# Attention and mixture-of-experts layer on one core: three fp32r passes for fp32 products, another order around them, and scatters in pairs

## The chip, the cores and the metric

The kernel runs on one core of a Trainium2 chip. The core has TensorE (PE: matmuls; PEld: its weight loads), VectorE (DVE), ScalarE (ACT), GpSimd (POOL) and SyncE (SP, which here issues DMAs), and 16 DMA engines. The engines run programs of their own and meet at semaphores. The metric is the device time of one execution in microseconds; lower is better.

## The reference

One pre-norm transformer block in fp32 on 4 x 1024 tokens of 256 values:

```python
x = x + attn(layernorm(x))      # 16 heads of 16, causal window of 64, softmax
x = x + ffn(layernorm(x))

# ffn(x): 8 experts of width 128, two chosen per token, plus a shared one of width 256
scores = sigmoid(x @ gate_w.T + lb_bias)
topw, topi = top_k(scores, 2);  topw = topw / (topw.sum(-1, keepdims=True) + 1e-08)
for e in range(8):
    m = topi == e
    wmean = (topw * m).sum() / maximum(m.sum(), 1)      # one weight for all of an expert's tokens
    y = silu(x @ gate[e].T) * (x @ up[e].T) @ down[e].T
    out = out + where(m.any(-1)[:, None], y * wmean, 0)
out = out + silu(x @ shared_gate.T) * (x @ shared_up.T) @ shared_down.T
```

## The kernel before

The program is written engine by engine; the order on each engine is the order in which its functions are called, and every hand-over is a semaphore. No scheduler moves anything. It has four stages.

**Sweep.** 16 groups of 256 tokens, each of 4 blocks of 64 queries (64 blocks in all). `step(g, ..., old, ahead)` does group g; iteration n works on three blocks at once. On PE it issues the scores of block b+1, the P·V product of block b-1 (`pv_of`, 16 pairs of small matmuls), a piece of the next group's projections (q in iteration 0, k in 1, v in 2), the row-maximum correction of block b (`shift_of`), the transposition of the maxima of b+1 (`maxima_T`), the transposition of the P·V result (`pvT_of`, which waits for ScalarE's copy `pv_copy`), the output projection of the group before (`wo_of`, iterations 1 and 2) and the transposition of o (`oT_of`). VectorE takes the maxima of b+1 out of PSUM, makes the negated maxima in two bf16 parts, and SyncE's queue loads them as a row (`load_mrow`, two DMAs) for `shift_of` of b+1. VectorE also does layer norms, residuals, o, and the router's ranking (`comparisons`, `ranks`) for a group two or three behind. GpSimd does the power of the variances (`rstd_of`), computes where each token's row goes (`places`), and from group 4 on scatters the rows of the group four behind to the experts' lists in DRAM: `scatter` issues four indirect DMAs in a row, 128 rows of 1032 bytes each. SyncE loads one set of feed-forward weights per step (`load_weights`).

**Epilogue.** The last groups are routed, the tile table (which expert has which of the 72 tiles) is made, and between that PE does the first ten units of the shared expert. A unit is `gate_up` (four products) and `down` (two) for 256 tokens and half of the shared width.

**Tiles.** 72 tiles of 128 rows; tile t has on PE: two transpositions of its rows, two products for gate and up, one transposition of the hidden values, one product for down, spread over four rounds (`rows_T` of t+2, `tile_gate_up` of t+1, `hidden_T` of t, `tile_down` of t-1). VectorE copies the transposed rows and multiplies, ScalarE does silu, copies the transposed hidden values and scales the result, GpSimd scatters it to `y_rows` in DRAM, one indirect DMA a tile.

**Tail.** The remaining 22 shared units; two rows per token come back from `y_rows` (`load_experts_rows`), GpSimd adds the two, VectorE adds them to `xs` (`combined`), SyncE stores the group.

All products are plain fp32. One product in the code is `eng.matmul(out, lhsT, rhs)` with 128x128 weights and 256 moving columns; the trace has two records for each. In the names of the trace, `ps` is PSUM, `wA` the attention weights (and in the tiles the transposed rows and hidden values), `wF` the feed-forward weights, `yT`, `zT` and `oT` the transposed activations, `probs` the softmax, `pvs` the copied P·V.

GpSimd's part of a step before the change:

```python
if g >= GPB:
    places(g - GPB, place)
    scatter(g - GPB, place)
...
if old:
    if g > GPB:
        eng.wait_ge(s_sc[(g - 1) % GPB], 64 * ((g - 1) // GPB))
    rstd_of(1, g)
```

## Time and profile before

| | |
|---|---|
| time, median of 3 runs | 613.49 us (612.69 to 614.48) |
| the profiled execution | 616.98 us, span from first to last instruction 615.2 us |
| PE matmul busy | 555.0 us, 90% |
| PE weight loads busy | 417.2 us, 68% |
| VectorE busy | 354.0 us, 58% |
| ScalarE busy | 289.5 us, 47% |
| GpSimd busy | 218.4 us, 36% |
| mean granted TensorE clock | 0.968 of full speed |
| chain that ended last | PE 71%, VectorE 13%, unknown queue 6%, ScalarE 4% |

A record of a matmul overlaps the next one, so busy time is the union of records; the distance between records in a stream is the cost of one. An interval in brackets behind an instruction is the time for which its engine sat idle before it, and behind the arrow stands what ended that.

### The profile page before, as it was taken

The page shows a single profiled execution, that of the slowest core. Times are in us where ns is not written, and L with a number is a line of the kernel's source. Part 1 is how long each engine was busy: PE and PEld are TensorE (multiplying, and loading weights), DVE is VectorE, ACT ScalarE, POOL GpSimd, SP SyncE. Part 2 cuts the span into 40 slices and gives each one's busy share as a digit, 9 for nine tenths or more (in the row PEclk, how much of TensorE's full clock was granted, in tenths as well). Part 3 has the DMA queues.
Part 4 walks back from the last instruction along what each step waited for, and adds up shares of the span by engine and source line. Part 5 has one row for each costly group of instructions (what it writes and reads, how often), then busy time and mean ns, then how long its engine had stood idle before and what let it go on. Part 6 is the DMA issues. An engine that isn't in the chain of part 4 may idle for free.

```text
span 615.2 us, 14456 instructions
## 1 busy us (share of the span) xinstructions
PE 555.0 (90%) x4969; PEld 417.2 (68%) x4969; DVE 354.0 (58%) x1084; ACT 289.5 (47%) x650; POOL 218.4 (36%) x384
## 2 busy tenths in 40 slices
PE   7699999989898898898898987898999999999995
PEld 4466766666566565565575664786888887868884
DVE  4456577666465575675665567268555554533454
ACT  3366665645445555455455563221555554541110
POOL 4000012342240431422413423662456555555620
PEclk9899999999798998999999999698999999999999
DMA  7400000210201101112101101115455554518753
GB/s 249 164 3 3 2 2 4 62 45 20 63 23 40 52 20 55 37 27 63 36 2 38 36 2 38 70 57 159 135 152 162 153 159 134 157 58 301 247 147 126
DMA packets 37862, 50.79 MB, mean 83 GB/s; under 512 B 9244, under 2 KB 28063, under 8 KB 37792
## 3 DMA queue, kind: packets, MB, share of 16 engines
q1 hardware_dynamic: 31264, 33.02, 17.7%
q0 software_dynamic: 6528, 16.86, 8.3%
q8 instruction: 42, 0.69, 0.5%
q14 instruction: 28, 0.23, 0.1%
HBM read 27.36 MB, written 23.27 MB: 82 GB/s over the span
## 4 chain that ended last, share of the span: by engine, by line
PE 71%; DVE 13%; another core or an unknown queue 6%; ACT 4%; issue 3%; DMA 2%; POOL 1%; DVEq 0%; SPq 0%; POOLq 0%; ACTq 0%
PE ps L774 10%; PE ps L694 7%; PE ps L525 6%; PE ps L491 5%; PE ps L791 5%; PE ps L576 5%; PE ps L511 5%; PE ps L501 4%; DVE rmax L997 4%; PE ps L704 3%; PE ps L554 3%; PE ps L562 3%; PE ps L536 3%; PE ps L766 2%
## 5 line engine op out<-in xcount | busy, mean ns | idle before, releaser
L997 DVE TRANSPOSE_TENSOR_REDUCE rmax<-ps 128x32 f32<-128x1024 f32 x64 | 79.5, 1242 | 62.8 <-PE ps L525 61.0
L459 POOL DMA_INDIRECT y_rows<-vm,dest x72 | 70.2, 976 | 63.5 <-issue 40.1
L367 POOL TENSOR_TENSOR rstd<-mv,epsb 128x2 f32<-128x2 f32 x32 | 6.2, 193 | 241.6 <-DVE mv L982 241.6
L868 ACT ACTIVATE probs<-ps 128x1024 f32<-128x1024 f32 x64 | 65.7, 1026 | 25.0 <-PE ps L541 25.0
L774 PE MATMUL ps<-wF,wA 128*128 x288 | 75.0, 383 | 0.5 <-DVE wA L1246 0.5
L422 POOL DMA_INDIRECT z_slots<-z,slot x64 | 64.7, 1011 | 29.4 <-issue 18.0
L525 PE MATMUL ps<-bd,kT 64*128 64x256 f32 x512 | 66.4, 380 | 0.0
L694 PE MATMUL ps<-zT,wF 128*128 128x256 f32 x256 | 62.4, 388 | 0.6 <-ACT vm L957 0.6
L874 ACT COPY pvs<-ps 128x256 f32<-128x256 f32 x64 | 23.8, 372 | 81.5 <-remote 42.5
L694 PEld LDWEIGHTS ps<-zT,wF 128*128 128x128 f32 x256 | 49.5, 195 | 7.8 <-ACT vm L957 1.0
L525 PEld LDWEIGHTS ps<-bd,kT 64*128 64x128 f32 x512 | 50.0, 191 | 5.0
L774 PEld LDWEIGHTS ps<-wF,wA 128*128 128x128 f32 x288 | 49.7, 192 | 5.0 <-issue 1.1
L1251 DVE TENSOR_TENSOR vt<-vt,ps 128x128 f32<-128x128 f32 x72 | 20.7, 288 | 53.7 <-ACT vt L946 51.4
L562 PE MATMUL ps<-identf,pvs 128*128 128x128 f32 x128 | 26.8, 293 | 23.1 <-ACT pvs L874 22.3
L1002 DVE TENSOR_REDUCE negm<-ps 32x32 f32<-32x128 f32 x64 | 17.8, 277 | 51.3 <-remote 26.7
L946 ACT ACTIVATE vt<-ps 128x128 f32<-128x128 f32 x72 | 20.0, 277 | 54.2 <-PE ps L774 48.8
L791 PE MATMUL ps<-wF,wA 128*128 x144 | 43.4, 384 | 0.1
L853 ACT ACTIVATE bd<-qs,cst 128x512 f32<-128x512 f32 x62 | 43.3, 725 | 0.0
L926 ACT ACTIVATE sg<-ps 128x256 f32<-128x256 f32 x32 | 12.2, 383 | 62.1 <-PE ps L694 60.9
L501 PE MATMUL ps<-yT,wA 128*128 128x256 f32 x128 | 41.0, 430 | 0.0
L957 ACT ACTIVATE vm<-ps,tile_w 128x256 f32<-128x256 f32 x72 | 34.1, 474 | 10.6 <-PE ps L791 3.7
L491 PE MATMUL ps<-yT,wA 128*128 128x256 f32 x128 | 37.9, 403 | 0.8 <-ACT yT L830 0.8
(160 smaller groups left out, 1095.5 us busy)
## 6 DMA issues: line engine op xcount, KB each, us to landing
z<-z_slots SPq DMA_DIRECT2D x72, 129.0 KB
bd<-y_rows SPq DMA_DIRECT2D x8, 512.0 KB, 7.4
out<-xs SPq DMA_DIRECT2D x16, 256.0 KB, 3.6
wF<-wffn SPq DMA_DIRECT2D x10, 384.0 KB, 3.3
xs<-x SPq DMA_DIRECT2D x7, 512.0 KB, 6.0
shift<-negs SPq DMA_DIRECT2D x128, 2.0 KB
z<-y_rows SPq DMA_DIRECT2D x4, 512.0 KB, 6.7
probs<-y_rows SPq DMA_DIRECT2D x4, 512.0 KB, 7.5
```

Source lines behind the costliest of these rows:

```text
L422: eng.indirect_dma_start(z_slots, bass.IndirectOffsetOnAxis(ap=slot[:, c, j, t:t + 1], axis=0), z[:, c, t, :], None, bounds_check=E * REGI ...
L459: eng.indirect_dma_start(y_rows, bass.IndirectOffsetOnAxis(ap=dest[:, m:m + 1], axis=0), yo[:, m, :], None, bounds_check=K * T - 1, oob_is ...
L491: mm = eng.matmul(bank(BANK_A)[:, m, :], wA[:, 0, k, m * P:(m + 1) * P], yT[:, k, :], start=k == 0, stop=k == KT - 1)
L501: mm = eng.matmul(bank(to)[:, m, :], wA[:, 1, k, m * P:(m + 1) * P], yT[:, k, :], start=k == 0, stop=k == KT - 1)
L525: mm = eng.matmul(S[n % 2][:, c, m * QH * WIN:(m + 1) * QH * WIN], kT[rows[c], par, m, n:n + 2, :].rearrange("p a c -> p (a c)"), bd[rows[ ...
L562: mm = eng.transpose(ps[:, PV, (KT + c) * P:(KT + c + 1) * P], pvs[:, c * P:(c + 1) * P], identf[:, :])
L694: mm = eng.matmul(bank(unit_banks[i % NU])[:, c, :], wF[:, E + e, (2 * k + c) * P:(2 * k + c + 1) * P], zT[:, g, k, :], start=k == 0, stop ...
L774: mm = eng.matmul(ps[:, m % 2, 0:2 * P], z1[:, m % 2, k * P:(k + 1) * P], weights(e, 2 * k * P, 2 * (k + 1) * P), start=k == 0, stop=k == ...
L791: eng.matmul(ps[:, 2 + m % 2, 0:D], hT[:, m % 2, :], weights(e, 4 * P, 6 * P), start=True, stop=True).then_inc(s_d1, 1)
L853: spread = eng.activation(bd[:, par, :, :, h, :], qs[:, :].rearrange("p (m n q) -> p m n q", m=KT, n=BPG), ACT.Copy, scale=const("quad")[: ...
L868: eng.activation(probs[:, n % 2, :], S[n % 2].rearrange("p a c -> p (a c)"), ACT.Exp, scale=HD ** -0.5).then_inc(s_P, 1)
L997: eng.tensor_reduce(rmax[:, n % 2, 0:32], S[n % 2].rearrange("p a (c q) -> p (a c) q", q=32), AX.X, ALU.max, apply_transpose=True).then_in ...
```

## The change

- **Splits.** Each fp32 operand of q, k, v, wo, gate/up and the tiles' down product is kept as two fp32r tensors: high, a rounding copy (ScalarE, `hi_of`, `oT_hi`, `rows_hi`, `hidden_hi`, `weights_hi`), and low, the difference (VectorE, `lo_of`, `oT_lo`, `rows_lo`, `hidden_lo`, `weights_lo`, `split_weights`). `product` then issues three matmuls: high·high, high·low, low·high. Transpositions, scores, P·V and the shared expert's down product (`wD`) stay plain fp32. The router's product becomes eight fp32r matmuls of 16 columns for a group, its halves are added by VectorE, and the bias is added in a step of its own.
- **Storage.** zT of each group now goes to DRAM (`store_zt`, 512 KB, SyncE) and is loaded again for the shared expert into five places (`load_zt`, ScalarE's queue). The feed-forward weights are loaded raw (`wraw_of`), split in steps 2 to 12.
- **Order.** PE issues `shift_of` before P·V; ScalarE runs exp before `pv_copy`. A group's four scatters are issued as two and two, the second pair behind `rstd_of(1, g)`. In the epilogue wo of the last group stands after half a `gate_up`, the tile table is made one tile per partition and spread by two small matmuls. In the tail `combined` is called by a table of turns.

```diff
                 def step(g, turn, place, par, old, ahead):
                     if g and g + 2 < NG:
                         rstd_of(0, g + 3)
                     if g >= GPB:
                         places(g - GPB, place)
-                        scatter(g - GPB, place)
+                        scatter(g - GPB, place, (0, 1))
                     if not ahead:
+                        scatter(g - GPB, place, (2, 3))
                         places(g - 3, (place + 1) % GPB)
                     if old:
                         if g > GPB:
                             eng.wait_ge(s_sc[(g - 1) % GPB], 64 * ((g - 1) // GPB))
                         rstd_of(1, g)
+                    if g >= GPB and ahead:
+                        scatter(g - GPB, place, (2, 3))
...
+                def product(out, lhsT, rhs, start, stop, skip=False):
+
+                    for n, (a, b) in enumerate(((0, 0), (0, 1), (1, 0))):
+                        mm = eng.matmul(out, lhsT(a), rhs(b), start=start and n == 0,
+                                        stop=stop and n == 2, skip_group_check=skip)
+                    return mm
...
                     for m in chunks:
                         for k in ks:
-                            mm = eng.matmul(bank(BANK_A)[:, m, :], wA[:, 0, k, m * P:(m + 1) * P], yT[:, k, :],
-                                            start=k == 0, stop=k == KT - 1)
+                            mm = product(bank(BANK_A)[:, m, :], lambda a: wA[:, a, 0, k, m * P:(m + 1) * P],
+                                         lambda b: yT[:, b, k, :], k == 0, k == KT - 1)
...
                             scores_of(b + 1, par2, n2, mask_first if first else window_mask)
+                        shift_of(b, g, n)
                         if n == 1:
                             eng.wait_ge(s_v, g + 1)
                         if old or n:
...
-                        shift_of(b, g, n)
...
+                def store_zt(G):
+                    eng.wait_ge(s_zTl, G + 1)
+                    eng.wait_ge(s_zTh, G + 1)
+                    dst = zT_dram[G] if isinstance(G, int) else zT_dram[bass.ds(G, 1), :, :].rearrange("o p c -> p (o c)")
+                    eng.dma_start(dst, f(zT[:, :, :, :]).rearrange("p a k c -> p (a k c)")).then_inc(s_zst, 16)
...
                         b = BPG * g + n
+                        exp_of(b, n, old == 0)
                         if old or n:
                             pv_copy(b - 1)
-                        exp_of(b, n, old == 0)
...
+                        if n == 3 and 2 <= g < NW + 2:
+                            w = g - 2
+                            eng.wait_ge(s_wf[w % 2], 16 * (w // 2 + 1))
+                            eng.copy(wF[0][:, weights_at(w), :], wraw_of[:, w % 2, :]).then_inc(s_wFh, 1)
...
+                def lo_of(dst, hi, src_bank, s_in, s_out, G):
+                    eng.wait_ge(s_in, G + 1)
+                    eng.tensor_tensor(dst, ps[:, src_bank, :].rearrange("p (a c) -> p a c", a=2), f(hi),
+                                      ALU.subtract).then_inc(s_out, 1)
...
+                        if old or n:
+                            oT_lo(b - 1, (n - 1) % BPG)
...
+                def rows_hi(t, q, m):
+                    eng.wait_ge(s_T, t + 1)
+                    after(eng, s_g1, t - 1)
+                    eng.copy(z1[:, m % 2, 0, :], ps[:, 4 + m % 2, 0:D]).then_inc(s_zh, 1)
...
-                def rows_copy(t, q, m):
-                    eng.wait_ge(s_T, t + 1)
-                    after(eng, s_g1, t - 1)
-                    eng.tensor_copy(z1[:, m % 2, :], ps[:, 4 + m % 2, 0:D]).then_inc(s_z1, 1)
+                def rows_lo(t, q, m):
+                    eng.wait_ge(s_zh, t + 1)
+                    eng.tensor_tensor(z1[:, m % 2, 1, :], ps[:, 4 + m % 2, 0:D], f(z1[:, m % 2, 0, :]),
+                                      ALU.subtract).then_inc(s_zl, 1)
...
-                    eng.wait_ge(s_wf, 16 * NW)
-                    gate_up(0)
                     oT_of(BPG * NG - 1)
-                    gate_up(1)
+                    eng.wait_ge(s_wFl, 2 * NW)
+                    eng.wait_ge(s_wD, 16)
+                    gate_up(0, (0,))
                     eng.wait_ge(s_lg, NG - 1)
                     wo_of(NG - 1)
+                    gate_up(0, (1,))
+                    gate_up(1)
...
-                for i in range(NG):
-                    for e in range(NS):
-                        if i < NG - GA:
-                            hidden_of(NS * (GA + i) + e)
-                    if 0 < i <= NG - GA:
-                        accumulate(GA + i - 1)
-                    combined(i)
+                turn_of = [max(5 * g // 4 + 3, 2 * (g - GA) + 3) for g in range(NG)]
+                for n in range(NS * (NG - GA)):
+                    hidden_of(NS * GA + n)
+                    if n % 2 and n > 1:
+                        accumulate(GA + (n - 3) // 2)
+                    for g in range(NG):
+                        if turn_of[g] == n:
+                            combined(g)
```

GpSimd in a step of the sweep from group 4 on (L401 to L414, later L447 to L460, are `places`; the rstd pairs are `rstd_of`). Before:

```order
L413 CAST slot<-picked 128x4
L414 COPY z<-picked 128x2
L422 DMA z_slots<-z,slot 33920x258 x4
L367 TENSOR_TENSOR rstd<-mv,epsb 128x2
L369 TENSOR_TENSOR rstd<-rstd,mhalf 128x2
L367 TENSOR_TENSOR rstd<-mv,epsb 128x2
```

Now:

```order
L459 CAST slot<-picked 128x4
L460 COPY z<-picked 128x2
L469 DMA z_slots<-z,slot 33920x258 x2
L413 TENSOR_TENSOR rstd<-mv,epsb 128x2
L415 TENSOR_TENSOR rstd<-rstd,mhalf 128x2
L469 DMA z_slots<-z,slot 33920x258 x2
L413 TENSOR_TENSOR rstd<-mv,epsb 128x2
```

The third and fourth scatter moved behind the rstd of the second layer norm, which waits for VectorE's statistics of the same step.

TensorE in iteration 1 of a step of the sweep (scores, P·V of the block before, the first k products, the shift, the transposed maxima). Before:

```order
L520 MATMUL ps<-identb,window_mask 128x512 x2
L525 MATMUL ps<-bd,kT 128x256 x4
L554 MATMUL ps<-probs,vm 32x64 x16
L501 MATMUL ps<-yT,wA 128x256
L541 MATMUL ps<-shift,onesb 128x512 x2
L536 MATMUL ps<-identf,rmax 128x128
L501 MATMUL ps<-yT,wA 128x256
L562 MATMUL ps<-identf,pvs 128x128 x2
L501 MATMUL ps<-yT,wA 128x256 x2
L576 MATMUL ps<-wA,oT 128x256 x2
L568 MATMUL ps<-identf,o 128x128
```

Now:

```order
L578 MATMUL ps<-identb,window_mask 128x512 x2
L583 MATMUL ps<-bd,kT 128x256 x4
L599 MATMUL ps<-shift,onesb 128x512 x2
L612 MATMUL ps<-probs,vm 32x64 x16
L524 MATMUL ps<-yT,wA 128x256 x3
L594 MATMUL ps<-identf,rmax 128x128
L524 MATMUL ps<-yT,wA 128x256 x3
L620 MATMUL ps<-identf,pvs 128x128 x2
L524 MATMUL ps<-yT,wA 128x256 x6
L524 MATMUL ps<-wA,oT 128x256 x6
L626 MATMUL ps<-identf,o 128x128
```

The shift moved ahead of P·V, and each product (one matmul in the program) became three.

VectorE in iterations 3 and 0 of a step, from o of the one to the maxima of the other (`stats` and `mv` are the layer-norm statistics). Before:

```order
L1015 TENSOR_TENSOR o<-ps,rden 128x128
L978 BN_STATS stats<-xs 128x6 x2
L982 BN_AGGR mv<-stats 128x2 x2
L1027 TENSOR_TENSOR logits<-ps,biasb 128x16
L997 TENSOR_REDUCE rmax<-ps 128x32
```

Now:

```order
L1133 TENSOR_TENSOR o<-ps,rden 128x128
L1096 BN_STATS stats<-xs 128x6 x2
L1100 BN_AGGR mv<-stats 128x2 x2
L1090 TENSOR_TENSOR yT<-ps,yT 128x512
L1138 TENSOR_TENSOR oT<-ps,oT 128x2x64
L1157 TENSOR_REDUCE logits<-ps 128x16
L1152 TENSOR_TENSOR wF<-wraw_of,wF 128x384
L1193 TENSOR_TENSOR slots<-ps,cst 128x16
L1115 TENSOR_REDUCE rmax<-ps 128x32
```

Three subtractions (yT, oT, half of the expert weights) now stand between o and the next block's maxima.

## Rows read from the trace of the kernel before

**Rows 1.** Windows: busy us (x instructions) per engine, PE clock, DMA share, GB/s
```profile
100.80:122.30 21.50, 20.85 (x245) 14.58 (x245) 14.93 (x48) 12.88 (x26) 7.70 (x17) 1.00 0.16 46
318.90:342.40 23.50, 20.57 (x246) 14.51 (x246) 14.94 (x48) 12.90 (x26) 7.63 (x18) 1.00 0.08 25
434.30:532.00 97.70, 96.35 (x532) 81.09 (x531) 51.47 (x178) 53.41 (x177) 57.18 (x59) 1.00 0.52 154
566.00:605.00 39.00, 39.00 (x183) 34.37 (x182) 18.83 (x30) 5.76 (x15) 16.11 (x13) 1.00 0.61 195
```

**Rows 2.** Timeline, PE: start, us, engine, line, operation, [idle before]; one per group
```profile
79.89 0.33 PE L536 MATMUL ps<-identf,rmax 128*128 128x128 f32 x1 [0.78 <-DVE rmax L997]
...
100.76 0.33 PE L536 MATMUL ps<-identf,rmax 128*128 128x128 f32 x1 [0.57 <-DVE rmax L997]
...
342.35 0.33 PE L536 MATMUL ps<-identf,rmax 128*128 128x128 f32 x1 [0.57 <-DVE rmax L997]
```

**Rows 3.** Timeline of 128 to 136 us: scatters, P·V and its copy
```profile
128.71 1.08 POOL L422 DMA_INDIRECT z_slots<-z,slot  x1 [0.81 <-POOL z L414]
...
130.50 0.65 PE L554 MATMUL ps<-probs,vm 128*32 128x64 f32 x32
...
132.64 0.97 POOL L422 DMA_INDIRECT z_slots<-z,slot  x1 [0.30 <-issue]
...
134.75 0.37 ACT L874 COPY pvs<-ps 128x256 f32<-128x256 f32 x1 [3.88 <-remote]
...
135.17 0.44 PE L562 MATMUL ps<-identf,pvs 128*128 128x128 f32 x2 [2.37 <-ACT pvs L874]
```

**Rows 4.** Waits of the whole run: us in total, times, longest
```profile
ACT pvs L874 <- remote: 42.5, 12, 3.9
```

**Rows 5.** Groups by form: output, inputs, count, busy us, mean ns, idle before
```profile
L774 PE MATMUL ps<-wF,wA 128*128 x288 | 75.0, 383 | 0.5 <-DVE wA L1246 0.5
...
L541 PE MATMUL ps<-shift,onesb 64*128 64x512 bf16 x128 | 25.2, 390 | 4.2 <-DMA shift<-negs 4.2
...
L874 ACT COPY pvs<-ps 128x256 f32<-128x256 f32 x64 | 23.8, 372 | 81.5 <-remote 42.5 <-PE ps L554 39.0
...
L1251 DVE TENSOR_TENSOR vt<-vt,ps 128x128 f32<-128x128 f32 x72 | 20.7, 288 | 53.7 <-ACT vt L946 51.4 <-issue 2.3
...
L1138 DVE TENSOR_TENSOR xs<-xs,ps 128x512 f32<-128x512 f32 x16 | 10.9, 684 | 2.7 <-PE ps L704 2.4
```

**Rows 6.** Timeline: one block on VectorE, and weight loads of the router's products
```profile
88.18 1.25 DVE L997 TRANSPOSE_TENSOR_REDUCE rmax<-ps 128x32 f32<-128x1024 f32 x1 [1.29 <-PE ps L525]
...
90.93 0.29 DVE L1015 TENSOR_TENSOR o<-ps,rden 128x128 f32<-128x128 f32 x1
...
101.44 0.52 PEld L591 LDWEIGHTS ps<-wG,zT 128*128 128x128 f32 x4
```

**Rows 7.** Timeline: the first shift of the sweep
```profile
23.23 0.61 PE L541 MATMUL ps<-shift,onesb 64*128 64x512 bf16 x2 [4.20 <-DMA shift<-negs]
```

**Rows 8.** Timeline: last block, last scatter, first loads of rows
```profile
384.62 0.37 PE L568 MATMUL ps<-identf,o 128*128 128x128 f32 x1 [1.48 <-DVE o L1015]
...
419.07 0.98 POOL L422 DMA_INDIRECT z_slots<-z,slot  x1 [0.31 <-issue]
...
423.11 2.51 SPq L330 DMA_DIRECT2D z<-z_slots  x5
```

**Rows 9.** Timeline: the first transposition of two tiles in a row
```profile
500.81 0.38 PE L766 MATMUL ps<-identf,z 128*128 128x128 f32 x2
...
502.43 0.38 PE L766 MATMUL ps<-identf,z 128*128 128x128 f32 x2
```

**Rows 10.** Timeline of the tail: two units, and the last additions
```profile
601.11 1.89 PE L694 MATMUL ps<-zT,wF 128*128 128x256 f32 x8
...
603.70 1.89 PE L694 MATMUL ps<-zT,wF 128*128 128x256 f32 x8
...
610.63 1.28 DVE L1276 TENSOR_TENSOR xs<-xs,probs 128x512 f32<-128x512 f32 x2
```

More of the change, by code:

```diff
@@ L17 @@
 F32 = mybir.dt.float32
+F32R = mybir.dt.float32r
 I32 = mybir.dt.int32
@@ L790, in tile_down @@
                     after(eng, s_y1, t - 1)
-                    eng.matmul(ps[:, 2 + m % 2, 0:D], hT[:, m % 2, :], weights(e, 4 * P, 6 * P), start=True, stop=True
-                               ).then_inc(s_d1, 1)
+                    product(ps[:, 2 + m % 2, 0:D], lambda a: hT[:, m % 2, a, :],
+                            lambda b: weights(e, b, 4 * P, 6 * P), True, True).then_inc(s_d1, 1)
                 def tile(q, m, first, last):
```

444 lines of the change are left out of this document (285 added, 159 removed).

## The prediction

> **What bounds the kernel now.** The page's busy table comes first: TensorE (PE) works for 90% of the span, VectorE for 58%. A mean over stages says little, so next come the windows. In a group of the sweep PE works 20.85 of 21.5 us early on and 20.57 of 23.5 later, with the same number of instructions; in the tiles it works 96.35 of 97.7, in the tail 39.00 of 39.00 [rows 1]. So PE sets tiles and tail, and in the sweep PE does, plus something that adds 2 to 4 us to the later groups. I date the groups by one transposition of the maxima that recurs in each: 79.89 to 100.76 is 20.87 us, and the ten groups from there to 342.35 take 24.16 each [rows 2].
>
> **What the later groups lose.** The timeline shows it. GpSimd issues a group's four scatters one after the other, from 128.71 to 133.61. PE starts a P·V product at 130.50, between them; its records last 0.65 us, so ScalarE's copy of the result is due at 131.2. It starts at 134.75, and PE, which waits for that copy, has idled for 2.37 us at 135.17 [rows 3]. This is one of 12 such waits, 42.5 us together [rows 4]; the copy comes 1.1 us after the last scatter's issue has ended. What holds PE's completion is not in the trace (the releaser is "remote"); that it begins with a P·V inside a run of scatters and ends with the run is what the rows show. In the tiles GpSimd scatters all the time and PE is not held [rows 1], so it is not scatters as such.
>
> **The change, part by part.** The sum is made against the profiled execution (616.98 us: the span of 615.2 and 1.8 around it), 3.5 above the median of 613.49; that difference carries over.
>
> (a) **Price of a product.** Today an fp32 product of 256 columns is two records, and eight records take 1.89 us: (1.89 - 0.38) / 7 = 0.216 each [rows 10], 0.43 a product. It becomes three fp32r passes, which no row shows. Cheap end: a pass streams like bf16, whose record of 512 columns lasts 390 ns, as long as one of 256 fp32 columns (383) [rows 5], so 256 columns in 0.107. Dear end: a pass costs what an fp32 record does, 0.216, either at its rate or because its weight load isn't hidden. That load takes (0.52 - 0.20) / 3 = 0.107 us in the router's products, which have 8 columns and so go at the pace of their loads [rows 6]. A product thus costs 0.32 to 0.65 us against 0.43, and breaks even at 0.143 a pass. I take 0.11 a pass, 0.33 a product, near the cheap end: wherever a row has 256 columns the load lies under the matmul before, and a load of 0.107 just fits under a pass of 0.107. Saving 0.10 a product.
> The Trainium skill (FP8 and Floating Point Precision, TensorE Precision Notes) says that true fp32 takes four passes through the array, and that reduced fp32 reads 4 bytes and truncates them. By it three passes for four give 0.32 us; no row of before can show it. The Trainium skill (TensorE: Matmul & The Clock Gate, LDWEIGHTS) puts a load at columns divided by 1.2 GHz, 107 ns here; the trace agrees. By it no pass with a load of its own goes under 0.107, which is the cheap end again.
>
> (b) **Sweep, PE.** Sixteen products a group (q, k, v, wo): 20.9 - 1.6 = 19.3 us.
>
> (c) **Sweep, VectorE.** The low halves are new work there. It is busy 14.93 us a group [rows 1]. Added: two subtractions of 128x512 from PSUM at 0.684 (yT, zT), four of 128x128 at 0.288 (oT) [rows 5], a bias addition of some 0.15: 2.7 us. In steps 3 to 12 also two of 128x384, between those sizes, 0.55 each: 1.1. That is 17.6, or 18.7. VectorE also loses time between dependent steps: from the start of the maxima at 88.18 to the end of o at 91.22 is 3.04 us [rows 6] for instructions that sum to 2.4, so 2.6 a group. Together 20.3 without the expert weights and 21.4 with them, both above PE's 19.3: **VectorE becomes the bound of the sweep**. I add 0.5, because it now waits in each block for ScalarE's half of oT. Three early groups at 19.7 (not all work has begun), ten at 21.9, three at 20.7: 340. Today the sweep runs from 23.23 [rows 7] to 384.62 [rows 8], 361.4 us. Minus 21.
> ScalarE gets a copy of 128x768 (about 0.8) in ten groups and works 13 of 23 us [rows 1]: covered. The zT stores, 512 KB a group on SyncE's queue behind the row maxima of block 1, have a block (5 us) before the next maxima, and weight loads of 384 KB stand in that place today: costed at nothing; if they run over, each us late costs one in up to 14 groups.
>
> (d) **Scatters in two pairs.** The first pair would end at 128.71 + 2 x 1.3 = 131.3. If PE is released 1.1 us after a run, at 132.4, the copy (0.37) ends at 132.8, which is when PE wants it (135.17 - 2.37). The second pair stands behind an rstd that needs block 2's statistics, so it falls into block 3, after that block's P·V and before the next. GpSimd works 8 of 23 us and has room. Shift and exp now stand ahead of P·V, so a held P·V doesn't hold exp. The stall goes; it is inside the 21 of (c), since without it today's groups would take 20.9.
>
> (e) **Prologue.** Splitting the weights delays q and k by 1.5 to 2.5 us, but the first shift waits 4.20 us for its DMA, behind the loads of x, in any case [rows 7]; 256 KB more stand in that queue. Plus 1.
>
> (f) **Epilogue.** The tiles' first rows are loaded at 423.11, when the last scatter, issued at 419.07, has landed [rows 8]. GpSimd is the chain: 16 scatters at 1.3 us fill 21 of the 38 us from 384.62, the placing between them most of the rest. The last wo product now comes after half a shared unit rather than two, which helps by at most 5; I take minus 3. The tile table's shorter steps end before that load in any case: nothing.
>
> (g) **Tiles.** A tile takes 502.43 - 500.81 = 1.62 us [rows 9], the stage 118.6 for 72. PE: minus 3 x 0.10 gives 1.32. GpSimd: one scatter, 1.28. ScalarE: today 53.41 / 60 = 0.89 [rows 1], and now the high half of the rows, a 128x256 copy of 0.37 [rows 5]: 1.26. VectorE: 0.86, less a little for the copy, plus 0.29: 1.15. Four engines within 0.2 of each other, all handing on by semaphores: I take 1.42, minus 15.
>
> (h) **Tail.** 22 units at 603.70 - 601.11 = 2.59 [rows 10], of which four of six products change: minus 0.4 x 22 = 9. Then, behind the last product, five additions of expert rows stand, until 611.9 [rows 10]; the new order leaves one: minus 2.5. The zT loads add some 3 MB to a tail that moves 195 GB/s [rows 1], and are asked for five groups ahead: covered, up to plus 4 if not.
>
> **Sum**: -21 + 1 - 3 - 15 - 11.5 = -49.5. Profiled 567.5, median **564.0 us**.
>
> **Rivals.**
> A, the forecast: 0.60, own range 548 to 580 (a product 0.32 to 0.36, a sweep group 0.7 either way, a tile 1.35 to 1.5).
> B, the scatter stall stays, so that this part doesn't do what it says: a pair still holds a P·V, or the new transfers do. For it: the trace doesn't name the blocker. Against: the first run of scatters, in the group after 100.76, had no P·V inside it and no such wait followed. 12 groups x 2.5 = 30 more: 594. Chance 0.15.
> C, **slower**: a pass costs what an fp32 record costs. For it: every fp32 record of this trace streams a column in 0.83 ns. Then a product is 0.65, and the sweep is PE-bound at 20.9 + 3.4 = 24.3 a group (+28), tiles +0.64 x 72 = 46, tail +19 - 2.5, epilogue +8, prologue +1: 713. In tiles and tail it decides from 0.143 a pass on. Against: two records for one product show that fp32 is split already, so the rate may belong to the split. Chance 0.12.
> D, VectorE is worse than its sum: its new waits for ScalarE stand ahead of the next maxima, on which the transposition, the maxima's DMA, shift and exp hang. From about 23.2 a group the sweep gains nothing: 585. Chance 0.13.
>
> **How the numbers follow.** The predicted time is A's. The range of 8 in 10 leaves out C and the far ends of A: 546 to 600. A measurement of this kernel tells about 0.3% (1.8 us) from no change. Faster: A, B, D, less a sliver, 0.87; within 0.3%: 0.01; slower: C, 0.12.
>
> **What would show it.** (a) fp32r records in a stream 0.107 to 0.12 apart; at 0.143 or more the forecast fails at its root. (c) VectorE above 85% in the sweep, PE waiting for it before the transposed maxima, groups at 21.9 in the middle and 20.7 at the end. (d) No copy of P·V waiting over 1.5 us, no idle 2.4 us of PE. (g) Tiles 1.42 apart, waits spread over three engines. (h) Units of 2.2 us and one addition after the last accumulation. Wrong would be: groups at 24, a halved clock in mid-sweep, or PE waiting for zT in the tail.

## The result and the profile after

The changed kernel takes 591.5 us (586.3 to 596.5), the kernel before 614.0 in the same runs: ratio 0.9605, 95% interval 0.9538 to 0.9672. The ratio leaves out the execution of 596.5, which was counted as slow. The time lies in the range that was given, near its far end. By the medians the gain is 22.5 us where the prediction's sum had 49.5, less than half of it; the profiled executions, on which the stages below rest, differ by 25.5 (591.49 against 616.98).

Five moments date the stages in every trace: the first shift, the transposition of o of the 63rd block, the first and the last transposition of hidden values in the tiles, and the end.

| us | before | after | change | forecast |
|---|---|---|---|---|
| prologue | 23.2 | 23.4 | +0.1 | +1 |
| sweep | 361.4 | 332.2 | -29.2 | -21 |
| epilogue | 46.0 | 47.6 | +1.6 | -3 |
| tiles | 117.7 | 129.8 | +12.0 | -15 |
| tail | 66.8 | 56.7 | -10.1 | -11.5 |

Four stages came out within some 8 us of their terms. The tiles missed theirs by 27 us, which is more than the whole error of 24 (49.5 - 25.5). The windows (columns as in [rows 1]) of a sweep group, the tiles and the tail of after:

```profile
225.71:246.44 20.73, 18.86 (x261) 15.11 (x262) 18.00 (x57) 13.61 (x27) 7.91 (x17) 1.00 0.24 73
405.00:530.00 125.00, 109.72 (x817) 98.37 (x816) 72.16 (x271) 77.81 (x271) 65.54 (x67) 1.00 0.46 138
540.00:580.00 40.00, 40.00 (x282) 38.19 (x281) 25.20 (x40) 6.52 (x17) 21.70 (x16) 1.00 1.00 369
```

PE works 109.7 of 125 us in the tiles, where it worked 96.35 of 97.7 before [rows 1]: it now waits, and no other engine is near full. In the sweep a group from 98.45 on takes 20.4 to 21.6 us, 20.73 in the best ones, instead of 23 to 26; VectorE works 87% of the one shown. The timeline of PE, one transposition of the maxima per group, answers to [rows 2]; behind it the waits of the whole run answer to [rows 4] (12 waits, 42.5 us):

```profile
204.97 0.33 PE L594 MATMUL ps<-identf,rmax 128*128 128x128 f32 x1 [0.87 <-DVE rmax L1115]
...
225.71 0.33 PE L594 MATMUL ps<-identf,rmax 128*128 128x128 f32 x1 [0.87 <-DVE rmax L1115]
```

```profile
ACT pvs L943 <- remote: 4.2, 2, 2.3
```

The tail's timeline answers to [rows 10]: gate/up of two units in a row, 2.30 us apart (2.59 before), and the addition that ends it.

```profile
562.87 1.79 PE L524 MATMUL ps<-yT,wF 128*128 128x256 f32 x12
...
565.17 1.79 PE L524 MATMUL ps<-wA,wF 128*128 128x256 f32 x12
...
586.43 0.69 DVE L1450 TENSOR_TENSOR xs<-xs,probs 128x512 f32<-128x512 f32 x1
```

**The granted clock.** The groups also differ by TensorE's clock. Windows of two neighbouring groups of the kernel before, and of two of the changed one:

```profile
270.67:294.14 23.47, 20.52 (x246) 14.46 (x246) 14.93 (x48) 12.86 (x26) 7.52 (x17) 1.00 0.14 42
294.14:318.90 24.76, 21.84 (x246) 15.47 (x246) 14.92 (x48) 13.08 (x26) 7.52 (x17) 0.93 0.07 23
```

```profile
225.71:246.44 20.73, 18.86 (x261) 15.11 (x262) 18.00 (x57) 13.61 (x27) 7.91 (x17) 1.00 0.24 73
246.44:267.83 21.39, 20.30 (x262) 15.95 (x262) 18.29 (x57) 13.67 (x27) 7.95 (x17) 0.92 0.23 69
```

A mean of 0.93 or 0.92 means that part of the group ran at the lower of the two levels, 1.2 GHz. It costs 1.3 us a group before and 0.7 after, with the same number of instructions on PE. Four of the eleven groups of after from 98.45 to 330.44 have such a stretch. What makes the clock fall there is not shown.

**What a long tile looks like.** The spacing of 1.62 us that [rows 9] showed was the same in nearly every tile of before. After, tiles come 1.41 apart in good stretches, and 20 of them take over 1.9, most of these 2.2 to 2.7; the mean is 1.83. The timeline of after from a scatter on: L509 is the scatter, L837 the transposition of rows on PE, L1042 ScalarE's high half of them, L1413 VectorE's low half, L524 x6 the gate/up passes that wait for it, L854 the transposition of hidden values, one per tile.

```profile
454.64 0.28 PE L854 MATMUL ps<-identf,vt 128*128 128x128 f32 x1
...
455.16 0.98 POOL L509 DMA_INDIRECT y_rows<-vm,dest  x1 [0.48 <-issue]
455.19 0.38 PE L837 MATMUL ps<-identf,z 128*128 128x128 f32 x2
...
456.12 0.28 PE L854 MATMUL ps<-identf,vt 128*128 128x128 f32 x1
...
456.56 0.37 ACT L1042 CAST wA<-ps 128x256 fp32r<-128x256 f32 x1 [0.32 <-PE ps L837]
...
456.96 0.42 DVE L1413 TENSOR_TENSOR wA<-ps,wA 128x256 fp32r<-128x256 f32 x1 [1.14 <-ACT wA L1042]
...
457.52 0.97 PE L524 MATMUL ps<-wF,wA 128*128 x6 [0.55 <-DVE wA L1413]
...
458.34 0.27 PE L854 MATMUL ps<-identf,vt 128*128 128x128 f32 x1
```

The transposition is done on PE by 455.57, yet ScalarE, which waits for it, starts at 456.56. The low half and the passes follow at once, and the tile takes 2.22 us (458.34 - 456.12) instead of 1.48.

A completion is the semaphore event that tells the other engines that an instruction has ended; it is called late here when it comes over 0.15 us after the instruction's end in the trace. Not every completion has an event in this trace (of the 69 transpositions of rows 15 have none), so the counts are of those that have one. In the tiles, 33 transpositions of rows ended between 0.33 and 1.30 us after the start of a scatter, and the completions of 29 of them came late. The late ones, 31 in the stage, were 0.8 us late in the mean, 25 us in all. Most came 1.4 to 1.7 us after the scatter's start. Others are late too: 37 of 112 completions of the tiles' products and 16 of 62 of the transposed hidden values. Over the whole run, 104 of PE's 342 completions that fell due within 2 us of a scatter's start were late, and none of the 474 others. No event of ScalarE or VectorE was late in the stage, nor in the run.

The runs fall into two sets by the time of the unaltered kernel before: 613 to 614 us in the result and beside `after_again`, `before_again`, `four_in_a_run` and `narrow_passes` ("the 614 set"), 579 to 581 beside all others ("the 580 set"). The sets go with the chip as far as the records name it: those four ran on one chip, number 8, and the 580 set on five others (13, 11, 6, 3 and 7); the chip of the result is not named. No chip is in both sets, so a property of that chip and a condition of its runs can't be told apart. Times are compared within a set.

### The profile page after: what moved, and what is told of

Same layout as the page of the kernel before. It is cut to its first block, busy times and chain, and to the rows that moved or that the text cites. A ratio compares the mean times of both kernels' runs of the same rounds, so it can differ in the third digit from the quotient of the medians.

```text
span 589.7 us, 16243 instructions
## 1 busy us (share of the span) xinstructions
PE 521.1 (88%) x5573; PEld 431.5 (73%) x5573; DVE 414.3 (70%) x1299; ACT 315.9 (54%) x736; POOL 222.4 (38%) x384
## 4 chain that ended last, share of the span: by engine, by line
PE 70%; DVE 19%; issue 5%; ACT 3%; another core or an unknown queue 1%; DMA 1%; SPq 0%; POOL 0%; ACTq 0%; DVEq 0%; POOLq 0%
PE ps L524 37%; PE ps L583 6%; PE ps L612 5%; PE ps L767 5%; DVE rmax L1115 4%; PE ps L837 3%; PE ps L594 3%; DVE stats L1096 2%; PE ps L620 2%; PE ps L578 2%; DVE xs L1145 2%; PE ps L599 2%; PE ps L535 2%; PE ps L854 2%; PE ps L650 2%
## 5 line engine op out<-in xcount | busy, mean ns | idle before, releaser
L524 PE MATMUL ps<-wF,wA 128*128 x648 | 106.8, 303 | 10.4 <-DVE wA L1413 7.1
L524 PEld LDWEIGHTS ps<-wF,wA 128*128 128x128 f32 x648 | 85.7, 189 | 20.3 <-issue 18.4
L509 POOL DMA_INDIRECT y_rows<-vm,dest x72 | 70.4, 978 | 79.6 <-ACT vm L1068 32.9
L469 POOL DMA_INDIRECT z_slots<-z,slot x64 | 64.7, 1010 | 28.2 <-issue 16.9
L524 PE MATMUL ps<-yT,wA 128*128 128x256 f32 x384 | 69.2, 314 | 1.6 <-DVE yT L1090 1.5
L524 PEld LDWEIGHTS ps<-yT,wA 128*128 128x128 f32 x384 | 55.4, 204 | 5.2 <-issue 2.9
L1413 DVE TENSOR_TENSOR wA<-ps,wA 128x256 fp32r<-128x256 f32 x72 | 30.5, 424 | 34.2 <-ACT wA L1042 27.2
L1020 ACT ACTIVATE vt<-ps 128x256 f32<-128x256 f32 x32 | 12.3, 383 | 63.7 <-PE ps L524 53.7
L1056 ACT ACTIVATE vt<-ps 128x128 f32<-128x128 f32 x72 | 20.3, 283 | 29.1 <-PE ps L524 21.4
L594 PE MATMUL ps<-identf,rmax 128*128 128x128 f32 x64 | 20.5, 321 | 17.0 <-DVE rmax L1115 13.2
L524 PE MATMUL ps<-wA,yT 128*128 128x256 f32 x192 | 33.8, 302 | 0.0
L767 PE MATMUL ps<-wD,vt 128*128 128x256 f32 x128 | 33.2, 385 | 0.4 <-DVE vt L1290 0.4
L1042 ACT CAST wA<-ps 128x256 fp32r<-128x256 f32 x72 | 26.8, 374 | 9.1 <-PE ps L837 8.4
```

Of the source, the lines that this page charges most:

```text
L469: eng.indirect_dma_start(z_slots, bass.IndirectOffsetOnAxis(ap=slot[:, c, j, t:t + 1], axis=0), z[:, c, t, :], None, bounds_check=E * REGI ...
L509: eng.indirect_dma_start(y_rows, bass.IndirectOffsetOnAxis(ap=dest[:, m:m + 1], axis=0), yo[:, m, :], None, bounds_check=K * T - 1, oob_is ...
L524: mm = eng.matmul(out, lhsT(a), rhs(b), start=start and n == 0, stop=stop and n == 2, skip_group_check=skip)
L594: eng.transpose(ps[:, RT, 0:P], rmax[:, (n or 0) % 2, :], identf[:, :]).then_inc(s_RT, 1)
L767: mm = eng.matmul(bank(2 + (g + GA) % 2)[:, t, :], hf[:, i % NU, t * P:(t + 1) * P], wD[:, e, :], start=e == 0 and t == 0, stop=e == NS - ...
L1413: eng.tensor_tensor(z1[:, m % 2, 1, :], ps[:, 4 + m % 2, 0:D], f(z1[:, m % 2, 0, :]), ALU.subtract).then_inc(s_zl, 1)
```

## Experiments

### The same kernels again, in both sets

The changed kernel unaltered, twice (`after_again` in the 614 set, `after_b` in the 580 set), and the kernel before for its trace.

> The changed kernel unaltered, once more, because the kernel before took 580.4 us in the runs of the first experiments and 614.0 in those of the result. Theory S (a slower and a quicker setting of the same chip type): where TensorE's completions are held during scatters, the kernel before takes 614 and the changed one 591; where they are not, before takes 580 and changed about 563 to 568 (sweep 327 to 329, tiles 106 to 110, tail 56.7). Rival N: the changed kernel takes 590 there too, its long tiles having nothing to do with held completions.

> The kernel before unaltered, for its trace. Theory S: if its time is about 580, its groups take 20.87 us with all four scatters in a run, no copy of P.V waits 2 us or more, and no completion of TensorE inside a scatter is late; if its time is about 614, the 12 waits are there. Rival: the 34 us between 614 and 580 lie elsewhere (clock, DMA, code loading).

> The changed kernel unaltered, beside the next three, so that all four stand on one chip. Where the kernel before takes 613 to 614, as in the result: 587 to 592, and 24 to 30 completions of the transposed rows in the tiles come 0.2 to 1.2 us late. Where it takes 580: 562 to 568, and none is late.

| | before | after | ratio (95% interval) |
|---|---|---|---|
| 614 set | 613.1 | 591.7 | 0.965 (0.958 to 0.973) |
| 580 set | 581.2 | 561.2 | 0.966 (0.963 to 0.968) |

`before_again` took 614.1 with the 12 waits of [rows 4] in place (42.6 us), so its expectation for 614 holds. The change is worth the same share in both sets, but not in the same stages. In the 580 set the changed kernel's stages are 23.7, 327.1, 45.3, 106.4 and 56.7. The timeline of `after_b`, a transposition of rows at the same place beside a scatter as above:

```profile
454.91 0.27 PE L854 MATMUL ps<-identf,vt 128*128 128x128 f32 x1
...
455.38 0.38 PE L837 MATMUL ps<-identf,z 128*128 128x128 f32 x2
455.42 0.97 POOL L509 DMA_INDIRECT y_rows<-vm,dest  x1 [0.45 <-issue]
...
455.95 0.36 ACT L1042 CAST wA<-ps 128x256 fp32r<-128x256 f32 x1
```

Here ScalarE starts 0.57 us after the start of the transposition, there 1.37. Of 62 transpositions of rows that ended in that part of a scatter none was late; no tile takes over 1.9 us, and the stage takes 106.4 instead of 129.8. The same holds for all traces: in each of the six of the 614 set 55 to 127 completions of PE were late, all of them due within 2 us of a scatter's start, and in each of the fourteen of the 580 set at most one, by 0.2 us. Theory S (one kernel, two settings, which differ in late completions of PE) is borne out so far. The tails, which hold only the last scatters, take 56.7 us in both. That the late completions make up the 23 us between the two tile stages is likely, since nothing else that was looked at differs, but no edit shows it: late completions of all kinds sum to 72 us there, and how much of that slack hid is not known.

### Pairs or a run of four

The changed kernel with the pairs undone (the diff), and the kernel before with the pairs alone.

```diff
-                        scatter(g - GPB, place, (0, 1))
+                        scatter(g - GPB, place)
                     if not ahead:
-                        scatter(g - GPB, place, (2, 3))
                         places(g - 3, (place + 1) % GPB)
...
-                    if g >= GPB and ahead:
-                        scatter(g - GPB, place, (2, 3))
```

> The changed kernel with one edit undone: a group's four scatters are issued in one run again. Where completions are held: the run again catches a P.V, 1.5 to 2.5 us in each of 10 to 12 groups, 15 to 30 us more than the changed kernel. Where they are not held: the same time as the changed kernel within 0.5%.

614 set: 624.8 us (618.5 to 627.4), 33 more than the changed kernel beside it and slower than the kernel before (ratio 1.014, 1.005 to 1.023). The sweep takes 367.1 instead of 332, the rest the same. The effect is larger than expected, and in kind as expected; waits and timeline (L469 scatter, L609 P·V, L940 its copy):

```profile
ACT pvs L940 <- remote: 26.8, 12, 2.8
```

```profile
249.97 0.97 POOL L469 DMA_INDIRECT z_slots<-z,slot  x1 [0.30 <-issue]
250.97 0.65 PE L609 MATMUL ps<-probs,vm 128*32 128x64 f32 x32 [0.35 <-DVE oT L1135]
251.25 0.97 POOL L469 DMA_INDIRECT z_slots<-z,slot  x1 [0.30 <-issue]
...
252.52 0.98 POOL L469 DMA_INDIRECT z_slots<-z,slot  x1 [0.30 <-issue]
254.71 0.37 ACT L940 COPY pvs<-ps 128x256 f32<-128x256 f32 x1 [2.72 <-remote]
```

So in the 614 set the pairs bring 35 us of the sweep. Not all of it is waiting: the mean granted clock of the whole run falls too, to 0.936 to 0.945 from 0.965 to 0.968 in `after_again`, and by the windows above a group with a stretch at the lower level costs 0.7 to 1.3 us. The two parts were not separated. Three passes without the pairs take 5.7 to 7.3 us more in the sweep than plain fp32 (367.1 against 361.4, and 359.8 in `before_again`).

> The kernel before with only the scatters changed: a group's four scatters as two pairs, the second behind the rstd of the second layer norm. Theory P (the pairs alone remove the stall): the 12 waits of ScalarE for P.V of up to 3.9 us go, the groups of the sweep take 21.3 to 21.8 instead of 24.16, time 585 to 590, which is all of the 29 us that the sweep of the changed kernel gained, so that three passes and low halves gained nothing net there. Rival O (the order is needed too: without shift and exp ahead of P.V a pair still holds a P.V): 600 to 614.

> The kernel before with its scatters in two pairs, meant for the same chip. If the pairs alone remove the stall: groups of 20.9 to 21.5 us, the sweep 328 to 335 instead of 361, 582 to 588, so that the sweep's gain of 29 us is the pairs' alone. If they need shift and exp ahead of P.V: 600 or more. If the kernel before takes 580 there: 580 again.

Both fell into the 580 set: 579.5 beside 580.4 (ratio 1.001, 0.997 to 1.004) and 578.6 beside 579.3 (0.998, 0.996 to 1.001). There the pairs do nothing, since there is no stall to remove: the copy of P·V never waits for "remote". The timeline has the groups at 20.87 us:

```profile
226.03 0.33 PE L540 MATMUL ps<-identf,rmax 128*128 128x128 f32 x1 [0.57 <-DVE rmax L1001]
...
246.90 0.33 PE L540 MATMUL ps<-identf,rmax 128*128 128x128 f32 x1 [0.57 <-DVE rmax L1001]
```

The first expectation, 585 to 590, took the 614 set for granted and is missed for that reason. The sweep is 327.5 us in this kernel and 327.1 in `after_b`. Three passes, low halves and the new order, without a stall to confuse them, gain nothing in the sweep: PE has less to do (18.8 us of a group instead of 20.3), but it waits for VectorE's maxima, and a group takes 20.73 us instead of 20.87. Its other stages (45.5, 114.2, 66.8) stand in for before's in the 580 set: tiles -7.8, tail -10.1, together nearly the whole 20 us there. Plain fp32 with pairs never ran in the 614 set, so how the sweep's 29 us there divide between the pairs and the new order is open; undoing the pairs alone costs more than all of it.

### Rows three tiles ahead

```diff
-                    if not (last and m >= 6):
-                        rows_T(*later(q, m, 2))
+                    if not (last and m >= 5):
+                        rows_T(*later(q, m, 3))
...
-                    after(eng, s_g1, t - 1)
-                    eng.copy(z1[:, m % 2, 0, :], ps[:, 4 + m % 2, 0:D]).then_inc(s_zh, 1)
+                    after(eng, s_g1, t - 3)
+                    eng.copy(rows1[m % 4][:, 0, :], ps[:, 4 + m % 2, 0:D]).then_inc(s_zh, 1)
```

(`rows1` is four buffers; `rows_hi` and `rows_lo` are moved in the same way.)

> The changed kernel with the rows of a tile transposed, and split in high and low, three tiles ahead instead of two (four buffers instead of two). Theory H: a held completion of the transposed rows now has a whole tile (1.4 us) of slack and costs nothing; what stays are held completions of gate/up and hidden values, with 0.5 to 0.7 us of slack each: 1.45 to 1.6 us a tile, time 564 to 575. Rival C, as a bound by the sum of the engines' handshakes: the chain rows, high, low, gate/up gets the same slack, so it too expects 1.41 to 1.5. Rival R (registers, loads): 1.8 a tile, 591.

> The kernel with rows split three tiles ahead, once more, now read against the changed kernel on the same chip. If completions are held there: theory H gives 1.5 to 1.6 us a tile instead of 1.77 to 1.83, so 16 to 23 us less than the changed kernel, 568 to 575. If the held completions matter wherever they fall: 1.75, at most 5 us less. If the chip holds none: within 1% of the changed kernel, around 561.

> Rows split three tiles ahead, meant for a chip on which the kernel before takes 613 to 614 and completions are late. Theory H (a held completion of the transposed rows has a tile of slack and costs nothing): 1.5 to 1.6 us a tile against 1.77 to 1.83, 568 to 575. If the held completions cost as much wherever they fall: 1.75, 586 or more. If the kernel before takes 580 there: 560 again.

> Rows split three tiles ahead, meant for a chip on which the kernel before takes 613 to 614. Theory H: 1.5 to 1.6 us a tile against the changed kernel's 1.77 to 1.83 there, 568 to 575. If a held completion costs as much wherever it falls: 1.75, 586 or more. If the kernel before takes 580 there: 559 to 560 again.

All four fell into the 580 set: 561.2, 560.2, 558.8 and 560.8 us, tiles 105.7 to 106.4. The first expectation, 564 to 575 by theory H, was for the 614 set. Beside it in one set of runs the changed kernel took 561.2 with the same ratio to before (0.9657 and 0.9656). Where no completion is late, more slack buys nothing. Rival C of these expectations (the engines' handshakes alone make the long tiles, 1.8 us each) is out by `after_b` already, whose handshakes are the same and whose tiles take 1.50. What the edit does where completions are late stays untested.

### Plain fp32 in the tiles

```diff
-                        mm = product(ps[:, m % 2, 0:2 * P], lambda a: z1[:, m % 2, a, k * P:(k + 1) * P],
-                                     lambda b: weights(e, b, 2 * k * P, 2 * (k + 1) * P), k == 0, k == KT - 1)
+                        mm = eng.matmul(ps[:, m % 2, 0:2 * P], z1[:, m % 2, k * P:(k + 1) * P],
+                                        weights(e, 1, 2 * k * P, 2 * (k + 1) * P), start=k == 0, stop=k == KT - 1)
```

> The changed kernel with its 72 tiles in plain fp32 again: one matmul a product, VectorE copies the transposed rows, no low halves in the tiles; scatters, order and everything outside the tiles as in the changed kernel (for the experts VectorE copies the weights where it subtracted). Theory H: the scatters run as often, but with the rows copied in one step the completion of the transposed rows has slack again, and the tile is PE-bound as before: 1.62 to 1.66 us a tile, the stage 118 instead of 129.8, time 579 to 581. Rival C expects the same 1.62. Rival R (the register loads of eight experts at once, or the loads of zT, make the long tiles): the long tiles stay, 590 or more.

> The kernel with plain fp32 in the tiles, once more, against the changed kernel on the same chip. If completions are held there: 1.65 us a tile as before the change instead of 1.77 to 1.83, the stage 8 to 12 us shorter, 579 to 583: plain tiles are then the better ones. If the chip holds none: tiles of 1.62 against 1.50, 5 to 9 us slower than the changed kernel, around 571.

> Plain fp32 in the tiles, meant for the same chip. Theory H: 1.65 us a tile, as before the change, 579 to 583, which is better than the changed kernel's 591. If the long tiles come from anything else that the change brought (register loads, zT): 1.77 or more, 590. If the kernel before takes 580 there: 568 to 571 again.

All three in the 580 set: 571.0, 567.7 and 568.8. The second stood beside the changed kernel and takes 6.5 us more (567.7 against 561.2). The first expectation, 579 to 581, was for the 614 set. Windows of the tiles, of `plain_tiles_c` and of `after_b`:

```profile
405.00:500.00 95.00, 95.00 (x527) 80.38 (x526) 51.32 (x176) 53.10 (x177) 57.15 (x59) 1.00 0.54 157
```

```profile
405.00:500.00 95.00, 93.25 (x754) 89.94 (x753) 69.76 (x252) 74.37 (x252) 61.11 (x63) 1.00 0.55 165
```

PE is full with 1.63 us a tile in plain fp32. With three passes GpSimd scatters 63 tiles in the time of 59: 1.50 us a tile. The stage takes 114.2 to 115.9 against 106.4. So the passes do gain in the tiles, 8 to 9 us, where completions are on time. This edit never ran in the 614 set; the plain tiles there are those of the kernel before, 117.7, against 125.8 to 130.6 in the four traces of that set with three passes.

### Ordinary stores for the tiles' scatters

```diff
-                    eng.indirect_dma_start(y_rows, bass.IndirectOffsetOnAxis(ap=dest[:, m:m + 1], axis=0),
-                                           yo[:, m, :], None, bounds_check=K * T - 1, oob_is_err=False
-                                           ).then_inc(s_ysc[m], 16)
+                    n = t % (K * T // P)
+                    eng.dma_start(y_rows[n * P:(n + 1) * P, :], yo[:, m, :]).then_inc(s_ysc[m], 16)
```

> The changed kernel with one edit: in the tiles GpSimd stores a tile's 128 rows to consecutive rows of y_rows with an ordinary DMA instead of scattering them (so the rows that the tail adds are the wrong ones; the bytes are the same). Theory H (holds): each scatter of GpSimd keeps back every completion of TensorE that falls between 0.33 and 1.4 us after its start, and the longer tiles (2.2 to 2.7 us beside 1.41) are the tiles in which such a completion is the one of the transposed rows. Then the tile stage goes from 1.83 to 1.41 to 1.45 us a tile, from 129.8 us to 102 to 105, and the time from 591.5 to 564 to 568. Rival C (coupling): ScalarE's high half and VectorE's low half one after the other make the long tiles by themselves: 1.8 a tile, 591. If an ordinary DMA issued by GpSimd holds completions as a scatter does, H also gives about 590, and the trace tells the two apart by the completions.

> The kernel that stores the tiles' rows with an ordinary DMA from GpSimd, once more, against the changed kernel on the same chip (the rows that the tail adds are the wrong ones). If completions are held there: theory H, in which the scatter holds them, gives 1.45 to 1.5 us a tile and 563 to 568; if something else holds them, 1.77 to 1.83 and 591. If the chip holds none: about 564, as in its first run.

> Ordinary DMAs of GpSimd in place of the tiles' scatters (the rows that the tail adds are the wrong ones), meant for the same chip. If the scatters hold the completions: 1.5 us a tile, 565 to 570. If what holds them is any DMA that GpSimd issues, or no DMA of GpSimd at all: 1.77 to 1.83, 588 to 592. If the kernel before takes 580 there: 561 to 564 again.

This kernel leaves out the placing of the rows, so that the tail adds wrong ones. 580 set three times: 564.0, 560.7, 562.1, tiles 108.2 to 108.6, beside 106.4 with scatters. The first time lies in the 564 to 568 that theory H gave, but by coincidence: the unaltered kernel takes 561.2 in this set. Where nothing is late the scatter costs the tiles nothing. In the 614 set every late completion fell due within 2 us of a scatter's start; whether the scatter itself holds it, or anything that GpSimd issues would, no run shows.

### What a pass costs

Second and third pass of the shared gate/up on 128 columns instead of 256, which leaves out the low parts of half of the tokens.

```diff
                     for n, (a, b) in enumerate(((0, 0), (0, 1), (1, 0))):
-                        mm = eng.matmul(out, lhsT(a), rhs(b), start=start and n == 0,
+                        c = slice(0, narrow if n else None)
+                        mm = eng.matmul(out[:, c], lhsT(a), rhs(b)[:, c], start=start and n == 0,
```

> The changed kernel with the second and third pass of each gate/up product of the shared expert cut to 128 of their 256 columns (so those low parts are added for half of the tokens alone). It prices what sets 0.12 us a pass. If the stream of columns sets it: 0.06 to 0.07 a narrow pass, a unit 2.30 - 8 x 0.055 = 1.86 us. If the weight load or a fixed cost of a matmul sets it: 0.107 to 0.12 a narrow pass, a unit 2.2 to 2.3.

590.7 us in the 614 set (one execution). PE's timeline, gate/up of two units:

```profile
560.39 1.66 PE L525 MATMUL ps<-yT,wF 128*128 128x256 f32 x12
...
562.61 1.67 PE L525 MATMUL ps<-yT,wF 128*128 128x256 f32 x12
```

A unit takes 2.22 us instead of 2.30. The two plain products of down are four records and take 4 x 0.215 = 0.86 of it, so twelve full passes take 1.44, 0.12 each, and with eight of them halved 1.36: a narrow one takes (1.36 - 4 x 0.12) / 8 = 0.11. Halving the columns saves 0.01 of 0.12 us, so a pass is bound by its weight load or another fixed cost, as the second expectation had it. The Trainium skill (TensorE: Matmul & The Clock Gate, LDWEIGHTS) puts the load of 128 columns at 107 ns; the 0.11 of this run agrees, but doesn't show that it is the load rather than another fixed cost.

### Later loads of zT

The kernel with rows three ahead, and the loads of zT for groups 5 to 9 put off from the end of the epilogue to the ninth tile.

```diff
-                    if i % NS == NS - 1:
+                    if i % NS == NS - 1 and i // NS not in (GA - 2, GA - 1):
                         load_zt(i)
...
+                    if q == 1 and m == 0:
+                        load_ahead()
```

> Rows three tiles ahead, and the loads of zT for groups 5 to 9, which the changed kernel issues around the first loads of rows, put off until the ninth tile. In the changed kernel 6.3 us lie between the first load of rows (393.67) and the first transposition of a tile (400.01), and 6.7 between the last scatter's issue (386.97) and that load; in the kernel before it was 3.6 and 4.0, with less in the queues. If the zT loads are what makes the difference: 2.5 to 5 us less in the epilogue, 555 to 558 where the kernel before takes 580, and with theory H 563 to 572 where it takes 614. Rival: the tail waits for zT that comes later (no: groups 5 to 9 have 100 us), or the row loads are slow for another reason: no difference from 560.

580 set: 565.0 (563.3 to 565.7) beside 580.2, slower than the 558.8 to 561.2 of the kernel without that edit; 555 to 558 was expected if the loads held up the epilogue. The epilogue takes 43.5 us, against 43.6 to 45.1 without the edit: those loads were not what made it longer. The tiles take 112.1 instead of 106; the timeline of `later_loads` and a window of it say why:

```profile
419.55 0.44 PE L839 MATMUL ps<-identf,z 128*128 128x128 f32 x2 [3.53 <-DMA z<-z_slots]
```

```profile
412.00:419.00 7.00, 4.02 (x34) 3.73 (x32) 3.35 (x13) 3.70 (x13) 4.42 (x5) 1.00 1.04 390
```

Five loads of 512 KB at once fill the DMA engines (share 1.04, 390 GB/s), and the rows of the next tiles arrive 3.5 us late behind them. Where they stood before, PE had shared units to do.

## Why the prediction was wrong, by its steps

**(a) Price of a pass: right in kind, small in size.** 0.12 us instead of 0.11, so a product is 0.36 instead of 0.33 and saves 0.07, not 0.10. It lies under the break-even of 0.143, and rival C (a pass like an fp32 record) is out. That it doesn't go with the columns is shown by `narrow_passes`; the weight load, which the prediction named, is the likely floor.

**(b), (c) Sweep: the number came out, the reason only half.** At the full clock PE works 18.8 to 19.3 us a group (forecast 19.3), VectorE 17.5 to 18.0 (forecast 17.6 to 18.7), and VectorE's maxima are what PE waits for (0.87 us in the rows above). The ten groups from 98.45 take 21.2 in the mean, 20.73 in the best, where 21.9 was forecast, so the half microsecond added for waits was too much. The forecast named a halved clock in mid-sweep as a sign of being wrong but had no term for it; the stretches at the lower level in four of these groups cost some 2.8 us (4 x 0.7), and those of before, 1.3 a group, are part of what the stall's groups lost beyond 20.9. That three passes buy the sweep nothing was in the forecast, not put so: "without it today's groups would take 20.9", and 20.87 is what they take.

**(d) Stall: right.** 12 waits became 2, and undoing the pairs brings 12 back and costs 33 us, some of it by the clock.

**(e), (f).** The prologue grew by 0.1, not 1. The epilogue was to lose 3 and grew by 1.6. The 3 us did go, up to the issue of the last scatter (31.4 us from the 63rd block, 34.5 before), but what follows took them back: the first load of rows follows the last scatter's issue by 6.7 us where it was 4.0 [rows 8] (386.97 and 393.67), and the first transposition of rows comes 6.3 us after that load where it was 3.6. The zT loads were the suspect and `later_loads` cleared those it moved; in the 580 set the epilogue takes 42.4 to 48.2 over all kernels with the change and 45.4 to 45.5 without. The cause stays open.

**(g) Tiles: the step that failed.** "Four engines within 0.2 of each other, all handing on by semaphores: I take 1.42, minus 15." The period came out: 1.41 to 1.44 in undisturbed stretches of both sets. That is partly luck. With the price of (a) PE's own tile is 1.62 - 3 x 0.07 = 1.41, not 1.32, and in `after_b` the chain that ended last lies 98% on PE between 405 and 500 us: in those stretches PE sets the period, and the 0.10 that the forecast added for handing on stood in for the dearer pass. The step fails at two points. First, two tiles in every eight take 1.7 to 1.9 (mean 1.50, `after_b`); they recur as the loads of eight expert registers do, which was not tested. By that the stage is 106.4 us, 4 more than the 102.7 that the term left. Second, in the 614 set the stage takes 23 us more again, with late completions of PE in it. The prediction had seen a held completion in the sweep and excluded it here: "In the tiles GpSimd scatters all the time and PE is not held". Of 259 completions of PE in the tiles of the kernel before, 14 were late, by up to 2.2 us. PE was hardly seen to wait for them, since a tile of that kernel had slack for it. Its timeline (L766 transposition of rows, L1246 VectorE's copy, L774 gate/up):

```profile
481.28 0.38 PE L766 MATMUL ps<-identf,z 128*128 128x128 f32 x2
...
481.69 0.42 DVE L1246 COPY wA<-ps 128x256 f32<-128x256 f32 x1
...
483.12 1.03 PE L774 MATMUL ps<-wF,wA 128*128 x4
```

The copy ends at 482.11, and the products that read it start at 483.12: 1.0 us of slack. After the change, high and low half stand one behind the other and the period is shorter: in `after_b` the low half, started 0.4 us after the high one, ends 0.2 to 0.3 before its passes. A completion that is up to 1.3 us late had next to no room to hide. The sum of busy times per tile, which the step used, can't show that; the length of the chain from one engine to the next against the period does.

One thing speaks against too simple a rule. In the kernel before, in the 614 set, 59 transpositions of rows (57 in `before_again`) also end in that part of a scatter, nearly all at 0.56 us, and only 5 (4) are late. So the place in the scatter alone does not decide. What does is open, and so is what the edits that met only the 580 set would do in the other. The failed step is thus this term: it left out that the rows' chain would lose its slack. That the rows' late completions cost the 23 us is inferred from the two sets and not shown by an edit.

**(h) Tail: right.** 2.30 a unit for 2.19 forecast: 22 x 0.29 = 6.4 instead of 9, and the rest, 3.7, comes behind the last unit, where 2.5 were forecast. PE waited for no load of zT, with the DMA share at 1.00.

**Rivals.** B (a pair still holds a P·V) came in 2 of its 12 waits (2.3 us at most); what it is about came in the tiles. D did not come. The time of 591.5 is B's 594 by coincidence.

## What to carry to other kernels

Where a step that was one instruction becomes two on two engines, compare the whole chain from producer to consumer with the period, and give it a buffer more before the period shrinks; busy times per engine don't show lost slack. A stall of unknown cause that a trace shows in one stage is to be expected in any other stage with the same ingredients as soon as its slack goes. And measure such a change on more than one chip: here the pairs had their worth in only one of the two sets, and the gain of three passes in the tiles showed only in the other. Look at the granted clock of single groups too, where a stage is made shorter by removing waits.

## What the runs showed of the hardware

- Completions of TensorE can come late within 2 us of the start of an indirect DMA that GpSimd issues: in the changed kernel in the 614 set 104 of 342, and none of the 474 others; up to 1.3 us late for the tiles' rows (29 of 33 between 0.33 and 1.30 us), up to 3.6 us in the sweep of the kernel before. In the 580 set none of 62 rows' completions was late (`after_b`). ScalarE's and VectorE's recorded completions are on time in both.
- An fp32r pass of 128x128 weights and 256 columns costs 0.12 us, with 128 columns 0.11; an fp32 matmul of 256 columns 0.43.
- The kernel before took 613 to 614 us in some runs and 579 to 581 in others. The first are those of the result and of chip 8, the second those of five other chips. Its sweep is 359.8 us in `before_again`, and that of `before_with_pairs`, the nearest trace of the other set, 327.5, so some 32 of the 34 us between the sets lie in the sweep.
- A group of the sweep with part of it at the lower clock (mean 0.92 to 0.93 granted) takes 0.7 us longer in the changed kernel and 1.3 in the one before.
- Five loads of 512 KB issued together delay loads of 129 KB behind them by 3.5 us, on another queue.
